# Decoder layer with eight ranked experts: the 128-row block moved to the end, the 184- and 152-row blocks put in a row

## The reference

```python
probs = softmax(x @ Wr.T)                     # 8 experts
vals, idx = top_k(probs, 2)                   # two experts a token
gate = one_hot(idx) weighted by vals / vals.sum()
h = silu(einsum('btd,efd->btef', x, W1))      # 512 -> 2048
y = einsum('btef,edf->bted', h, W2)           # 2048 -> 512
out = einsum('bte,bted->btd', gate, y)
x = layernorm(x + out)
```

## Time and profile before

| what | value |
|---|---|
| median of 3 runs | 630.79 us (627.56 to 632.09) |
| the profiled execution | 627.21 us, its span 625.5 us |
| mean granted TensorE clock in it | 0.997 |
| TensorE, VectorE, ScalarE, POOL busy | 98%, 71%, 54%, 24% of the span |
| HBM read and written | 92.17 MB and 19.03 MB |
| DMA rate over the span | 179 GB/s |

### The profile page before, as it was taken

The page is one execution under the profiler, slowest core; times in us unless marked ns, Lnnn a source line. Parts: engine busy times, 40 slices in busy tenths (PEclk is TensorE's granted clock), DMA queues, the critical chain, the costliest instruction groups (busy, mean ns, idle before and its releaser), DMA issues.

```text
span 625.5 us, 9835 instructions
## 1 busy us (share of the span) xinstructions
PE 611.9 (98%) x3886; PEld 533.1 (85%) x3886; DVE 443.2 (71%) x612; ACT 339.6 (54%) x443; POOL 147.5 (24%) x136
## 2 busy tenths in 40 slices
PE   8999999999999999999999999999999999999995
PEld 7699978879978888789888888889998889888994
DVE  4575636545268995868886786785886669889886
ACT  4754532115325567455565564655665569565755
POOL 2160000000648785304710000000000000183451
PEclk9999999999999999999999999999999999999998
DMA  8994006004800001302976656666476488898522
GB/s 291 402 374 189 1 15 288 1 0 139 317 1 2 2 1 69 135 2 88 354 266 205 225 210 208 218 227 219 175 268 221 169 269 300 293 353 291 187 71 106
DMA packets 27223, 111.83 MB, mean 179 GB/s; under 512 B 3928, under 2 KB 5464, under 8 KB 17578
## 3 DMA queue, kind: packets, MB, share of 16 engines
q1 hardware_dynamic: 21956, 97.00, 42.9%
q0 software_dynamic: 3536, 11.11, 5.2%
q10 hardware_dynamic: 1686, 3.10, 1.5%
HBM read 92.17 MB, written 19.03 MB: 178 GB/s over the span
## 4 chain that ended last, share of the span: by engine, by line
PE 78%; DVE 9%; DMA 3%; ACT 3%; POOL 3%; issue 2%; SPq 1%; POOLq 0%; ACTq 0%
PE bank L2053 14%; PE bank L1725 13%; PE bank L1727 13%; PE bank L1726 13%; PE bank L2045 7%; PE bank L2097 4%; POOL routed L648 3%; PE bank L1760 2%; PE bank L2091 2%; PE bank L1782 2%; DVE probs L1240 2%; DMA x<-in_x_tok 2%; DVE row_sum L1252 1%; DMA routed<-x,row 1%; DVE row_max L1246 1%
## 5 line engine op out<-in xcount | busy, mean ns | idle before, releaser
L2053 PE MATMUL bank<-xg_cat,whi 128*128 128x480 f32 (+3 forms) x512 | 153.6, 364 | 0.0
L1451 DVE TENSOR_TENSOR wlo<-raw,whi 128x2048 fp32r<-128x2048 f32 x54 | 122.8, 2288 | 24.6 <-ACT whi L955 24.5
L2045 PE MATMUL bank<-xg_cat,wlo 128*128 128x240 f32 (+3 forms) x512 | 113.3, 262 | 0.0
L955 ACT ACTIVATE whi<-raw 128x2048 fp32r<-128x2048 f32 x54 | 101.9, 1907 | 16.2 <-PE bank L1727 7.2
L2045 PEld LDWEIGHTS bank<-xg_cat,wlo 128*128 128x128 f32 x512 | 94.6, 189 | 5.1
L2053 PEld LDWEIGHTS bank<-xg_cat,whi 128*128 128x128 f32 x512 | 89.1, 189 | 5.8
L900 ACT ACTIVATE hidden<-hidden 128x480 f32<-128x480 f32 (+3 forms) x64 | 34.7, 553 | 78.1 <-DVE hidden L1467 78.0
L1725 PE MATMUL bank<-whi,h_cat 128*120 128x512 f32 (+1 forms) x176 | 70.0, 397 | 0.0
L1727 PE MATMUL bank<-whi,h_cat 128*120 128x512 f32 (+1 forms) x176 | 69.5, 395 | 0.0
L1726 PE MATMUL bank<-wlo,h_cat 128*120 128x512 f32 (+1 forms) x176 | 69.4, 395 | 0.0
L1467 DVE TENSOR_TENSOR hidden<-bank,cross 128x480 f32<-128x480 f32 (+3 forms) x64 | 36.8, 585 | 29.7 <-ACT cross L893 29.7
(11 more groups left out here) (287 smaller groups left out, 1316.7 us busy)
## 6 DMA issues: line engine op xcount, KB each, us to landing
raw<-in_ffn_pieces SPq DMA_DIRECT2D x64, 1024.0 KB, 5.2
raw<-in_pieces SPq DMA_DIRECT2D x11, 1024.0 KB, 11.1
routed<-zeros SPq DMA_DIRECT2D x27, 256.0 KB, 4.9
expert_out<-zeros SPq DMA_DIRECT2D x15, 256.0 KB
xg<-routed POOLq DMA_DIRECT2D x8, 240.0 KB, 5.9
expert_out<-y_sb ACTq DMA_DIRECT2D x8, 240.0 KB
x<-in_x_tok SPq DMA_DIRECT2D x1, 1536.0 KB, 9.7
out<-x SPq DMA_DIRECT2D x6, 256.0 KB, 2.1
```

Of the source, the lines that this page charges most:

```text
L955: act.activation(whi[slot][:], raw[slot][:], ACT.Copy)\
L1451: dve.tensor_tensor(wlo[slot][:], raw[slot][:], f(whi[slot][:]), ALU.subtract)\
L2045: pe.matmul(o[:, 0:c], w_l[:, k, ft * P:(ft + 1) * P], xg_cat[:, k, 0, 0:c], start=False, stop=False)
L2053: mm = pe.matmul(o.rearrange("p (x c) -> p x c", x=2), w_h[:, k, ft * P:(ft + 1) * P], xg_cat[:, k, :, 0:c], start=(k == 0), stop=(k == KD ...
```

## The change

The order becomes `LATE` = (2, 5, 6, 3, 4, 7): 240, 184, 152, 240, 240, 128 rows. The 152-row block stands third, in the short form and with held weights, right behind the 184-row block; the 128-row block is the last. The final block uses `through_w2` in one group, so its result lies in one PSUM bank by rows: `feat_sum`, `feat_turned`, `y_cross` and the four-part splits go, one copy and one subtraction over 512 columns take their place, and `share_t` has one part, turned once, in the late block 3. `add_final` has two matmuls a tile. The share adds are given other places in VectorE's queue: eight in the block before the last (five before), ten in the last one (sixteen before), and the last three, for tiles 4 to 6, in the tail ahead of the gated add of their tile.

```diff
 CT = -(-CMAX // P)
 CE = CAPS[1]
-LATE = (2, 5, 3, 7, 4, 6)
+LATE = (2, 5, 6, 3, 4, 7)
...
 WARM_TURNED = 4
 WARM_SPLIT = 3
-SHARE_IN = 2
-HELD = (1,)
-SHORT = (3,)
-OUT_BANK = (4, 5, 6, 7, 0, 1, 2)
+SHARE_IN = 3
+HELD = (1, 2)
+SHORT = (2,)
+OUT_BANK = (5, 6, 7, 0, 1, 2, 3)
 ON_POOL = (0, 2, 4)
...
-                    pool.wait_ge(share_mm, 2)
+                    pool.wait_ge(share_mm, 1)
                 if i >= NPICK:
...
-            def share_out(part):
-
-                act.wait_ge(share_mm, part + 1)
-                k = HF
-                act.activation(share_t[0:k, part, :], bank[0:k, 6:8, :].rearrange("p b c -> p (b c)")[:, 0:T], ACT.Copy)\
+            def share_out():
+
+                act.wait_ge(share_mm, 1)
+                act.activation(share_t[0:CF, :], bank[0:CF, 6:8, :].rearrange("p b c -> p (b c)")[:, 0:T], ACT.Copy)\
                    .then_inc(share_out_done, 1)
...
-                short_units(g, 1)
+                if held(g, 1):
+                    cross_half(g, 1, 0)
+                    cross_half(g, 1, 1)
+                    results_turned(g)
+                    short_units(g, 1, crossed=True)
+                else:
+                    short_units(g, 1)
                 hi_ahead(g, 3)
                 hi_ahead(g, 4)
                 short_units(g, 2)
                 hi_ahead(g, 5)
+                short_units(g, 3, turn=not final)
                 if not final:
                     hi_ahead(g, 6)
-                short_units(g, 3, turn=not final)
-                if not final:
...
-            for j in range(KD):
-                act.wait_ge(yt_mm, j + 1)
-                act.activation(y_cross[:, j, :], bank[:, 4 + j, CF:2 * CF], ACT.Copy).then_inc(yt_crossed, 1)
-                if j:
-                    final_high(j - 1)
-            final_high(KD - 1)
+            act.wait_ge(y_out[1], rows_out(FINAL))
+            act.wait_ge(final_mm, 1)
+            act.activation(final_hi[0:CF, :], bank[0:CF, 4, :], ACT.Copy).then_inc(final_read, 1)
             for t in range(TILES):
                 r = rows(t)
                 act.wait_ge(mean3, t + 1)
-                act.activation(pick_buf[t][0:r, :], x[0:r, t, :], ACT.Square, bias=less_mean[0:r, t:t + 1],
+                act.activation(pick_buf[3 + t % 6][0:r, :], x[0:r, t, :], ACT.Square, bias=less_mean[0:r, t:t + 1],
                                accum_out=ssq3[0:r, t:t + 1]).then_inc(ssq_done, 1)
                 act.wait_ge(ssq_done, t + 1)
                 act.activation(std3_col[0:r, t:t + 1], ssq3[0:r, t:t + 1], ACT.Sqrt, scale=1.0 / D,
...
+            def results_summed(g):
+
+                c = CAPS[LATE[g.n - 1]]
+                dve.wait_ge(y_apart, HELD.index(g.n - 1) + 1)
+                dve.tensor_tensor(features(c), bank[:, 4:4 + KD, 0:c], apart(c), ALU.add).then_inc(y_read[1], 1)
+
...
                 short_sums(g, 0)
                 short_low(g, 0)
                 lo_ahead(g, 1)
+                if held(g, 1):
+                    results_summed(g)
                 short_sums(g, 1)
                 lo_ahead(g, 2)
...
                 short_sums(g, 2)
                 lo_ahead(g, 4)
                 short_low(g, 2)
+                hidden_sum(g, 3, 0)
                 lo_ahead(g, 5)
-                short_sums(g, 3)
+                hidden_sum(g, 3, 1)
                 xg_halves(after(g))
+                short_low(g, 3)
                 lo_ahead(g, 6)
-                short_low(g, 3)
                 lo_ahead(g, 7)
             def gathering_block(g):
...
                 lo_ahead(g, 1)
+                if held(g, 1):
+                    results_summed(g)
                 lo_ahead(g, 2)
...
                 hidden_sum(g, 2, 0)
                 add_shares(0, 1)
                 hidden_sum(g, 2, 1)
-                add_shares(1, 2)
                 hidden_halves(g, 2)
                 lo_ahead(g, 5)
+                add_shares(1, 3)
                 lo_ahead(g, 6)
                 hidden_sum(g, 3, 0)
-                add_shares(2, 3)
+                add_shares(3, 4)
                 hidden_sum(g, 3, 1)
                 xg_halves(after(g))
                 hidden_halves(g, 3)
+                add_shares(4, 6)
                 lo_ahead(g, 7)
-                add_shares(3, 5)
-
-            def feat_sum(j):
-
-                dve.wait_ge(yt_crossed, j + 1)
...
             def final_block(g):
                 lo_ahead(g, 0)
-                add_shares(5, 6)
                 short_sums(g, 0)
-                add_shares(6, 8)
                 short_low(g, 0)
+                add_shares(8, 9)
                 lo_ahead(g, 1)
-                add_shares(8, 10)
                 short_sums(g, 1)
+                add_shares(9, 10)
                 lo_ahead(g, 2)
                 short_low(g, 1)
-                add_shares(10, 12)
+                add_shares(10, 11)
                 lo_ahead(g, 3)
-                add_shares(12, 14)
+                add_shares(11, 12)
                 short_sums(g, 2)
                 lo_ahead(g, 4)
                 short_low(g, 2)
                 lo_ahead(g, 5)
-                add_shares(14, 16)
+                add_shares(12, 14)
                 short_sums(g, 3)
-                add_shares(16, 17)
+                add_shares(14, 15)
                 short_low(g, 3)
-                add_shares(17, 19)
-                feat_sum(0)
-                add_shares(19, 20)
-                feat_sum(1)
-                final_low(0)
-                feat_sum(2)
-                final_low(1)
-                add_shares(20, 21)
-                feat_sum(3)
-                final_low(2)
-                final_low(3)
+                add_shares(15, 17)
+                add_shares(17, TILES * 2 + LATE_FROM)
+                dve.wait_ge(final_read, 1)
+                dve.tensor_tensor(final_lo[0:CF, :], bank[0:CF, 4, :], f(final_hi[0:CF, :]), ALU.subtract)\
+                   .then_inc(final_split, 1)
             first_low(1)
...
                 r = rows(t)
+                if t >= LATE_FROM:
+                    add_shares(2 * TILES + t, 2 * TILES + t + 1)
+                    dve.wait_ge(share_done, 2 * TILES + t + 1)
                 dve.wait_ge(add_mm, t + 1)
                 return step(dve.scalar_tensor_tensor(x[0:r, t, :], bank[0:r, OUT_BANK[t], :], gate_f[0:r, t:t + 1],
...
                     pe.wait_ge(y_read[isinstance(g, Late)], g.n + 1 if isinstance(g, Late) else g)
-                if isinstance(g, Late) and g.n in HELD + (FINAL,):
-                    feat_w2(q, piece_slot(g, j), cap(g)).then_inc(g2_mm[1], 1)
+                if held(g):
+                    feat_w2(q, piece_slot(g, j), cap(g), HELD.index(g.n - 1) + 1 if q == 0 and held(g, 1) else 0).then_inc(g2_mm[1], 1)
                 else:
                     through_w2(g, q, piece_slot(g, j), cap(g)).then_inc(signal(g2_mm, g), 1)
-            def feat_w2(q, slot, c, final=False):
+            def feat_w2(q, slot, c, behind=0):
                 w_h, w_l = wh(slot)
                 for j in range(KD):
+                    if behind and j == 2:
+                        pe.wait_ge(y_back, behind)
                     o = bank[:, 4 + j, 0:2 * c]
                     dj = slice(j * P, (j + 1) * P)
...
+            def share_turned():
                 pe.wait_ge(holders_done, 1)
-                k = HF
                 for t in range(TILES):
                     r, at = rows(t), t % 4 * P
-                    mm = pe.transpose(bank[0:k, 6 + t // 4, at:at + r], holders[0:r, t, part * k:part * k + k],
-                                      ident[0:r, 0:r])
+                    mm = pe.transpose(bank[0:CF, 6 + t // 4, at:at + r], holders[0:r, t, :], ident[0:r, 0:r])
                 mm.then_inc(share_mm, 1)
...
+                    share_turned()
                 through_w1(g, 2)
                 own_w2(g, 1)
-                if share:
-                    pe.wait_ge(share_out_done, 1)
-                    share_turned(1)
                 through_w1(g, 3)
                 if not final:
                     if share:
-                        pe.wait_ge(share_out_done, 2)
+                        pe.wait_ge(share_out_done, 1)
                     turn_rows(after(g))
                 own_w2(g, 2)
...
             pe.wait_ge(w_lo_late, LATE_PIECES - AHEAD)
             pe.wait_ge(h_split[1], 4 * len(LATE))
-            feat_w2(3, piece_slot(Late(FINAL), PER), CF, final=True)
-
-            def add_final(t, a, s, first, last):
+            through_w2(Late(FINAL), 3, piece_slot(Late(FINAL), PER), CF).then_inc(final_mm, 1)
+
+            def add_final(t, a, first):
                 r = rows(t)
-                k = HF
-                return pe.matmul(bank[0:r, OUT_BANK[t], :], share_t[0:k, s, t * P:t * P + r], a[0:k, s, :],
-                                 start=first, stop=last)
-
-            pe.wait_ge(yt_done, KD)
-            keep_warm(7, WARM_SPLIT)
-            pe.wait_ge(final_read, KD)
-            for t in range(2):
```

(19 more changed lines are left out.)

63 lines of the change are left out of this document (13 added, 50 removed).

## The result

The changed kernel takes 633.22 us in the median of twelve runs (630.21 to 636.03), the kernel before 629.75 in twelve runs beside it (626.97 to 632.18). The ratio is 1.0061, with a 95% interval of 1.0034 to 1.0088: slower by 2 to 5.5 us. Forecast were +2.7 and 633.5. The profiled execution took 633.16 (span 631.4), so it stands at the median, where that of before (627.21) was among the fastest.

The account below looks back on a forecast made before the run. TensorE, busy 98% of the span, was taken to bound the kernel until the last block is multiplied. The terms 6.2 - 6.8 + 2.5 - 1.6 + 2.4 = +2.7 us took the median 630.79 to 633.5, range 629.0 to 637.0.

Parts of the forecast that it names:

- Part 1, the order: Ahead of the last block: 152 rows in place of 128 lengthen W1, W2 and transposes, one holder turn goes; +6.2 us.
- the new queue work: 152-row block: ScalarE's apart copy and copy back, VectorE's sum; taken as covered by earlier W2 steps, 0 to +1 us.
- The rival that put a hole here: 152-row block: late sum, waiting transposes or held banks leave a new hole; +1 to +2 us, 635, chance 0.06.
- Part 2, the walk through VectorE's queue: Last block: TensorE work falls 6.8 us, but VectorE's late low half stalls TensorE 2.5 us before the last W2.
- S: Start of the last block, forecast 6.2 us later than 571.5; times within that block are counted from it.
- The clock rival: Stall before the last W2: idleness halves TensorE's clock for what follows; +6.8 us, 637.6, chance 0.09.
- Part 3: From the last W2 to the first gated add: 1.9 us in place of 3.54; -1.6 us.
- Part 4: Tail: share adds ahead of the gated adds of tiles 4 to 6 delay the end by +2.4 us; late gathers hidden.
- the 3.6 us between the two: Whole kernel before the change: profiled execution 627.21 us against the three-run median 630.79; the offset was kept for the forecast.
- the sum of +2.7: Whole kernel: 6.2 - 6.8 + 2.5 - 1.6 + 2.4 = +2.7 us, with the clock at 1.00 through it.

Follow-up runs that it names:

- e2: Changed kernel with share adds 9 to 11 moved ahead of the second sums and 12 to 17 after the last pair of sums; 628.76 us, ratio 1.0016.
- e8: Changed kernel with share adds 12 and 13 moved from ahead of the last pair of sums to behind it; 629.39 us, ratio 1.0004.
- e4: Changed kernel with all seven adds of late results ahead of the tail, instead of three in it; 631.22 us, ratio 1.0038.
- e10: Changed kernel with six filler matmuls in the routing; 634.15 us, ratio 1.0075 to the kernel before.
- e3: Changed kernel without the three share adds in the tail (tiles 4 to 6); 630.87 us, ratio 1.0011.
- e11: Changed kernel with six filler matmuls in the routing and eleven in front of the last low half; 632.23 us, ratio 1.0064.
- the packed kernels: Changed kernel with share adds packed where VectorE idled and fewer in the tail: e5 at 628.6 us, e6 at 630.65 us.
- e5: Changed kernel with share adds packed where VectorE idled, two in the tail, scaling of tiles 1 and 3 on POOL; 628.6 us, ratio 0.9992.
- e6: e5 with share 19 also ahead of the last split and the 152-row block's held results summed before its second weight split; 630.65 us, ratio 0.9997.
- e9: Kernel before the change with six filler matmuls in the routing; 628.3 us, ratio 0.998.
- e1: Changed kernel with eleven filler matmuls in front of the wait for the last low half; 632.42 us, ratio 1.0054.
- e7: e6 with six filler matmuls between the last tiles' routing steps; 626.72 us, ratio 0.9965.
- e12: e7 with share 13 behind the last sums, 14 to 18 behind the low half, 19 back in the tail; 627.74 us, ratio 0.9977.

## Why the prediction came out as it did

- *Part 1, the order (+6.2).* Measured +6.5 at the start of the last block, with the first late block 0.2 earlier, so +6.7 over the late blocks (198.11 to 204.82). Of the 0.5 above the forecast 0.4 is one hole. The W1 step of the 152-row block that starts at 463.27 takes 4.42 in place of 4.03, since TensorE's turn of the held results waits for VectorE's sum:

```profile
463.27:467.69 4.42, 4.17 (x34) 3.96 (x33) 3.35 (x3) 3.68 (x3) 0.00 (x0) 1.00 0.59 226
467.69:471.70 4.01, 4.01 (x33) 4.01 (x34) 3.06 (x3) 2.88 (x6) 0.00 (x0) 1.00 0.79 273
```

```profile
464.51 2.29 DVE L1440 TENSOR_TENSOR wlo<-raw,whi 128x2048 fp32r<-128x2048 f32 x1 [1.01 <-ACT whi L953]
...
466.72 0.92 DVE L1482 TENSOR_TENSOR y_sb<-bank,cross 128x736 f32<-128x736 f32 x1
...
467.69 0.75 PE L2104 MATMUL bank<-ident,y_sb 128*92 128x128 f32 x5 [0.25 <-DVE y_sb L1482]
```

  I costed the new queue work at nothing, with 0 to +1 as its bounds. The rival that put a hole here said that each VectorE step had over 1 us in hand. This one had none: the sum stood behind a weight split that had itself waited 1.01 for ScalarE. Its size was 0.4, not the rival's 1 to 2.
- *Part 2, the walk through VectorE's queue.* Forecast: second sums at S + 13.7, last sums at 28.6 to 29.3, low half 30.5 to 31.1, last W2 due at S + 28.6, stall 2.5. Measured: 13.7, 28.8, 30.7 to 31.4, 28.8, 2.66. The method, one queue added up in program order from one anchor that hangs on another engine, is good to 0.3 us over 17. e2 and e8 show that its cause, too, was the right one.
- *The clock rival (0.09).* Its mechanism is what most executions without a fall in the routing show (five of seven runs of the changed kernel, by their mean clock), and the step that priced it is the one that failed. I had it decide from a stall near the 3.1 us of the one fall seen, above my stall of 2.5. The fall came 1.96 us after the last matmul of a gap of 2.66. In e4 it came after 2.1, in e10 at 612.07, 3.26 after the gap's start and with the last W2 already running, in e3, whose clock had fallen in the routing, not at all. Its price was too high: no longer stall belonged to it (2.66), the link to the first gated add grew by 0.1 and not 0.5, and its share of the last W2 varies (2.4 us more in the changed kernel, 1.3 in e4, 1.6 in e10). e10 against e11 gives 1.9 us, the gap between the changed kernel's lower and middle group 2.0. The chance should have been nearer to one in two, at about 2 us over the forecast, still under the 1% of 6.3. The Trainium skill (TensorE: Matmul & The Clock Gate, Part 1) says that the moment at which the clock changes varies from run to run, and gives its figures for the rise. The three falls here, after 1.96, 2.1 and 3.26 us of the same stall, show that the moment of the fall varies too.
- *Part 3 (-1.6).* Measured -1.5: `final_hi` 0.60, `final_lo` 0.69, 2.02 in all against 1.9, part of it at the low clock. The forecast's terms stand.
- *Part 4 (+2.4).* 8.44 - 6.08 = 2.36; e3 without the adds has 6.07. That the late gathers are hidden was right: no share add of the changed kernel waits for a DMA; the packed kernels ask sooner and have to wait. Share 18 stands 42.9 us into the block in the changed kernel and 32.0 in e5, where it waits 0.30; share 19 waits 0.63 in e6, 33.2 into the block.
- *From the profiled execution to the median.* The forecast carried the 3.6 us between the two over unchanged. The runs show what they are: the kernel before has a second group of runs, by their mean clock and by e9 with the clock down in the routing, and its profiled execution was of the first. That group is in both kernels, so carrying it over was fair. The median of before was 629.75 here and not 630.79, and the change +3.5 and not +2.7; that the forecast of 633.5 is right to 0.3 is luck in part, because these two went opposite ways. The two profiled executions differ by 5.9, not 2.7. Executions with no fall at all, 627.5 on average for five of before and 630.4 for two of after, differ by 3.0, which is the case that the sum of +2.7 describes.

## What to carry to other kernels

When a block is made shorter on the bounding engine, count the side engine's queue in program order from the last point where it waited, and put every operation that nobody needs yet behind the one that the bounding engine needs next: here each add of 0.74 us ahead of the last pair of sums was 0.74 of stall. The one between those sums and the low half was hidden behind ScalarE's work (VectorE still waited 0.48 for the high half), and behind the low half adds were free until the split of the results. A stall on TensorE is priced twice, its own length and a chance of a halved clock on what follows; a few dummy matmuls in it take the second away where the first can't be helped. And where the runs of a kernel fall into groups, find the stretch that parts them before reading small ratios: a median moves with how many runs fell into which.

## What the runs showed of the hardware

- The granted clock fell with no idleness behind it that the records show. In the routing stretch it went to 0.50 at about 272 us in some executions of every kernel without fillers, while TensorE, by the records, had no gap over 0.3 us and only small matmuls; that costs 4 to 5 us. The traces of e1, e3, e6 and e8 show it; for the kernel before, whose long runs were never profiled without fillers, it is inferred from their mean clock (0.986 to 0.992). The Trainium skill (TensorE: Matmul & The Clock Gate, Part 1) names idleness in its table of states, and says in the text beside it that the level follows how busy the engine has been; this case shows a fall with no idle stretch. Six extra matmuls of 128 columns took nearly all of it away (e7, e9), for 0.8 us each time.
- The two falls seem to exclude each other. Of the four profiled executions with the full stall and no fillers in it, three ran the routing at 1.00 and fell in the stall or just behind it (changed, e4, e10); the fourth (e3) fell in the routing and held 1.00 through the stall. The runs agree: the mean clock of the changed kernel's upper group (0.984 to 0.986) is that of e1's upper group (0.983 to 0.986, but for one run at 0.989), in which the stall is filled. 13 us at half clock are 0.010 of the span, the fall in the stall with 6.8 us is 0.005, and the group without either has 0.993. None of the changed kernel's twelve runs is as low as both together would make it (0.978, an estimate from these rows). That the one shifts the moment of the other is likely by that, but was not tried.
- Left open: why the late blocks of e9, e10 and e11 are 0.7 to 0.8 us longer than without the routing's fillers and those of e7 and e12 are not, and what decides whether an execution falls in the routing.
